# Two recurrent layers with mixtures of experts on one core: output product, linear product, decays and keys in other places of the order

## The reference

```
# layer 1
s  = linear attention of xn: q, k = elu(.)+1, 16 heads of 64; kv = k^T v; (q kv) / (q ksum); @ Wout + bout
x2 = xn + softmax attention of rmsnorm(xn): 16 heads of 8, 4 groups of k and v, rope, causal; @ wo
m  = x2 + sum over the top 2 of 8 experts of w2(silu(w1 h) * (w3 h)) * weight,   h = rmsnorm(x2)
x  = x + s * silu(m)
# layer 2
q, k = l2 normalized; alpha = sigmoid(xn Wg + bg); chunks of 64 tokens:
la = cumsum(log(max(alpha, 1e-6)));  decay = exp(mean la_i - mean la_j) * tril
o  = ((q k^T) * decay) v + (q exp(la)) S;   S = S * exp(la_end) + (k exp(la_end - la))^T v
y  = xn + o Wo;  s = y + gelu(layernorm(y) W1 + b1) W2 + b2
m  = top 1 of 8 experts: relu(xn W1e + b1e) W2e + b2e
x  = x + s * silu(m)
```

## Time and profile before

| | us |
|---|---|
| time, median of 3 runs | 2266.91 (2261.11 to 2269.20) |
| profiled execution | 2266.75 |
| its span in the profile | 2265.0 |
| PE busy | 1846.0 (81%), 23060 matmuls |
| PEld busy | 1306.2 |
| DVE busy | 1238.1 (55%) |
| ACT busy | 1026.2 (45%) |
| POOL busy | 214.9 (9%) |
| mean granted PE clock | 0.919 |

### The profile page before, as it was taken

How to read it: one execution, slowest core, us unless ns; L and a number is a source line. 1 busy time by engine, 2 the same in 40 slices (tenths; PEclk the granted TensorE clock), 3 DMA queues, 4 the chain that set the end, 5 groups by cost and what they waited for, 6 DMA issues and landing times.

```text
span 2265.0 us, 61259 instructions
## 1 busy us (share of the span) xinstructions
PE 1846.0 (81%) x23060; PEld 1306.2 (58%) x23060; DVE 1238.1 (55%) x3454; ACT 1026.2 (45%) x2306; POOL 214.9 (9%) x235
## 2 busy tenths in 40 slices
PE   6999999998989999957788777887888888888652
PEld 4555555556666666635556555655556665655652
DVE  5566666665666656635446544655545655554412
ACT  2444444443555445534554355444554444455332
POOL 0000000000000000020011011100111100110022
PEclk9888889998998989969989999999999999999987
DMA  3222222222122211230221112110111111111374
GB/s 128 78 86 86 86 86 86 90 87 65 60 66 67 67 49 57 75 107 23 64 67 43 55 57 75 44 39 23 56 58 59 59 38 48 48 46 47 103 241 125
DMA packets 97602, 160.99 MB, mean 71 GB/s; under 512 B 14729, under 2 KB 66057, under 8 KB 94090
## 3 DMA queue, kind: packets, MB, share of 16 engines
q1 hardware_dynamic: 88170, 135.05, 18.2%
q0 software_dynamic: 9248, 23.17, 3.3%
HBM read 96.45 MB, written 61.69 MB: 70 GB/s over the span
## 4 chain that ended last, share of the span: by engine, by line
PE 57%; ACT 14%; DVE 12%; issue 11%; SPq 3%; DMA 1%; another core or an unknown queue 1%; POOL 1%; DVEq 0%; ACTq 0%; POOLq 0%
PE psum L907 5%; PE psum L977 4%; PE psum L775 3%; PE psum L897 3%; PE psum L946 3%; PE psum L1218 3%; PE psum L797 3%; PE psum L999 2%; PE psum L1109 2%; PE psum L992 2%; PE psum L1056 2%; PE psum L1080 2%; PE psum L806 2%; PE psum L1147 2%; PE psum L1207 2%
## 5 line engine op out<-in xcount | busy, mean ns | idle before, releaser
L1436 ACT ACTIVATE pts<-psum 128x512 f32<-128x512 f32 x192 | 99.0, 603 | 179.8 <-PE psum L946 179.8
L1901 DVE TENSOR_REDUCE mneg<-psum 128x2 f32<-128x512 f32 (+1 forms) x192 | 119.1, 683 | 57.0 <-PE psum L926 35.2
L682 POOL DMA_INDIRECT rows<-h,recA x64 | 61.8, 965 | 909.6 <-DVE recA L1664 777.5
L797 PE MATMUL psum<-txT,wt 128*128 128x128 f32 x864 | 124.2, 290 | 5.0 <-ACT txT L1319 4.9
L907 PE MATMUL psum<-wa,xT_s 128*128 128x512 f32 x256 | 118.7, 606 | 2.2 <-DVE mneg L1901 2.2
L797 PEld LDWEIGHTS psum<-txT,wt 128*128 128x128 f32 x864 | 113.5, 204 | 10.2 <-ACT txT L1319 6.7
L1066 PE MATMUL psum<-xT_s,wa 128*128 128x256 f32 x512 | 117.5, 383 | 0.0
L706 POOL DMA_INDIRECT rows<-xn,recC x32 | 32.7, 1023 | 884.2 <-DVE recC L2087 762.4
L1066 PEld LDWEIGHTS psum<-xT_s,wa 128*128 128x128 f32 x512 | 94.7, 190 | 25.4 <-issue 13.8
L2015 DVE TENSOR_SCALAR reg<-psum 128x512 f32<-128x512 f32 x16 | 11.1, 692 | 159.2 <-PE psum L1103 159.1
L806 PE MATMUL psum<-wt,tg 128*128 128x128 f32 x528 | 82.3, 288 | 14.4 <-DVE tg L1631 14.4
(11 more groups left out here) (276 smaller groups left out, 4542.8 us busy)
## 6 DMA issues: line engine op xcount, KB each, us to landing
wt<-in_wB SPq DMA_DIRECT2D x84, 384.0 KB, 2.9
outs<-pbd SPq DMA_DIRECT2D x16, 1024.0 KB, 7.0
wt<-in_wD SPq DMA_DIRECT2D x24, 578.0 KB, 3.5
wa<-in_wD SPq DMA_DIRECT2D x15, 578.0 KB, 3.5
tx<-rows SPq DMA_DIRECT2D x132, 64.0 KB, 2.9
outs<-ty SPq DMA_DIRECT2D x132, 64.0 KB, 1.6
rows<-pbd SPq DMA_DIRECT2D x64, 128.0 KB, 1.8
rows<-pbd SPq DMA_DIRECT2D x8, 1024.0 KB, 3.9
```

What stands on the lines that cost most here:

```text
L797: last = mm(bank(f"th{j}")[:, c * P:(c + 1) * P], view[s][:, c * P:(c + 1) * P], txT[:, s, :], start=True, stop=True)
L1436: af(pT[:, n, :], bank(f"e{n}"), ACT.Exp, scale=float(HD) ** -0.5).then_inc(*frees(f"e{n}"))
L1901: ins = v.tensor_reduce(mneg[:, int(n >= 4), col:col + hs], sc, AX.X, ALU.max, negate=True)
```

## The change

Layer 1. The product `wo` with the addition that gives x2 goes from the end of an element to the next one: on PE between `v9` and the k products, on DVE between the copy of v9 and the second pair of queries. A new semaphore `aT_ready` stands for the scaled sums, and x2_ready belongs to stage G. The first scores go ahead of h turned, the v products ahead of the gate. Behind the third scores PE does the linear product first, then the turned maxima, the first numerators, transposed scores 1, tile step 3, transposed scores 2, the second numerators. DVE adds the linear product's bias before the maxima, and divides the second numerators behind the choice and the norm. ACT takes the second set of exponentials ahead of tile step 3.

Layer 2. The logarithms (`decays`) stand right behind z's exponentials, ahead of tile step 4. The key products `lk` of an element are issued in the tail of the element before, behind f0 and f1 and ahead of tile step 5. Their squares are taken by ACT in the new `first_k()`, behind the reload of the table after the gelus, and the copies are now made by DVE, in the new `keys_turned()`, behind the decay means. The sums of squares wait for both.

The list of bank uses follows the new orders. The diff, cut to its core:

```diff
 # PE, layer 1
+            def attention_output():
+                if "G" not in now["stages"]:
+                    return
+                pe.wait_ge(*given("aT_ready", 0))
+                pe.wait_ge(*emptied("wo"))
+                for t in range(NT):
+                    for r in range(GR):
+                        last = mm(bank("wo")[:, t * P:(t + 1) * P], aT[:, r, t * P:(t + 1) * P], woR[:, r, :], start=(r == 0), stop=(r == GR - 1))
+                last.then_inc(*fills("wo"))
...
                 last.then_inc(*fills("v9"))
+                attention_output()
                 tokens("k", INNER)
-                h2_turned()
                 pe.wait_ge(*given("rope_ready"))
                 scores(0)
+                h2_turned()
+                tokens("v", 2 * INNER)
                 gate()
-                tokens("v", 2 * INNER)
...
                 scores(2)
+                linear_output()
+                maxima(1)
                 pe.wait_ge(*given("q0_ready"))
                 numerators(0)
-                linear_output()
-                maxima(1)
+                scores_T(1)
+                tile_step(3)
+                scores_T(2)
                 numerators(1)
-                tile_step(3)
-                scores_T(1)
-                scores_T(2)
...
-                pe.wait_ge(*read_out("pn1"))
...
                 tile_step(7)
 # PE, layer 2
-                products("lk", INNER)
                 tile_step(0)
                 pe.wait_ge(*given("sq_done", 0))
-                pe.wait_ge(*given("sk_done", 4))
-                for j in range(4):
-                    pe.wait_ge(*read_out(f"lk{j}"))
+                pe.wait_ge(*given("sk_done", 0))
+                pe.wait_ge(*given("kT_ready", 0))
...
+                if "P" in now["stages"]:
+                    products("lk", INNER)
                 tile_step(5)
 # ACT, layer 1
                 outputs_turned(1)
+                scores_T(1)
                 tile_step(3)
-                scores_T(1)
                 scores_T(2)
 # ACT, layer 2
+            def first_k():
+                if "P" not in now["stages"]:
+                    return
+                for j in range(4):
+                    act.wait_ge(*filled(f"lk{j}"))
+                    af(sqK[:, 2 * j:2 * j + 2, :], bank(f"lk{j}").rearrange("p (a n) -> p a n", a=2), ACT.Square).then_inc(*signals("sk_done"))
...
-                for j in range(4):
-                    act.wait_ge(*filled(f"lk{j}"))
-                    src = bank(f"lk{j}").rearrange("p (a n) -> p a n", a=2)
-                    af(sqK[:, 2 * j:2 * j + 2, :], src, ACT.Square).then_inc(*signals("sk_done"))
-                    af(kT[:, 2 * j:2 * j + 2, :], src, ACT.Copy).then_inc(*frees(f"lk{j}"))
...
                 z_products(0)
                 z_products(1)
+                decays(0)
+                decays(1)
                 tile_step(4)
                 first_q(0)
                 rstd("ln2", small[:, 1:4:2], small[:, 4:6], 1.0, eps)
                 for j in range(1, 4):
                     first_q(j)
-                decays(0)
-                decays(1)
...
                 act.preload_act_table_set("natural_log_exp_and_others")
+                first_k()
                 tile_step(5)
 # DVE
+            def keys_turned():
+                if "P" not in now["stages"]:
+                    return
+                for j in range(4):
+                    dve.wait_ge(*given("sk_done", j + 1))
+                    v.tensor_copy(kT[:, 2 * j:2 * j + 2, :], bank(f"lk{j}").rearrange("p (a n) -> p a n", a=2)).then_inc(*frees(f"lk{j}"))
+                dve.wait_ge(*read_out("lk3"))
+                dve.sem_inc(*signals("kT_ready"))
...
+            def attention_output():
+                if "G" not in now["stages"]:
+                    return
+                dve.wait_ge(*filled("wo"))
+                dve.wait_ge(*given("recA_stored", 1, 16))
+                v.tensor_tensor(x2[:, :, :], xk[:, :, :], tok(bank("wo")[:, 0:N]), ALU.add).then_inc(*frees("wo"))
+                dve.wait_ge(*read_out("wo"))
+                dve.sem_inc(*signals("x2_ready"))
...
-                v.tensor_copy(xk[:, :, :], xn[:, :, :]).then_inc(*signals("dve_chain"))
...
-                h2_scaled()
+                attention_output()
+                v.tensor_copy(xk[:, :, :], xn[:, :, :]).then_inc(*signals("dve_chain"))
                 queries(1)
                 head_stats()
+                h2_scaled()
                 maxima(0)
-                gate_taken()
...
+                gate_taken()
...
                 maxima(2)
+                linear_output()
                 maxima_added(1)
                 divided(0)
-                linear_output()
-                divided(1)
                 tile_step(3)
                 choose()
                 head_norm()
+                divided(1)
                 rows_given()
...
                 decay_means(0)
                 decay_means(1)
+                keys_turned()
                 tile_step(5)
```

More of the change, by code:

```diff
@@ L118, in uses_in_order @@
         names += [f"te{t}{c}" for t in range(NT) for c in range(2)]
-        names += [f"lk{j}" for j in range(4)]
         tile_step(0)
@@ L1051, in attention0 @@
                 tile_step(6)
-                pe.wait_ge(*read_out("pn1"))
-                pe.wait_ge(*emptied("wo"))
-                for t in range(NT):
-                    for r in range(GR):
-                        last = mm(bank("wo")[:, t * P:(t + 1) * P], aT[:, r, t * P:(t + 1) * P], woR[:, r, :], start=(r == 0), stop=(r == GR - 1))
-                last.then_inc(*fills("wo"))
                 tile_step(7)
```

40 lines of the change are left out of this document (22 added, 18 removed).

## The result

The changed kernel took 2148.06 us (median of 4 runs, 2147.29 to 2151.40), the kernel before beside it 2264.01: 0.950 of it, 95% interval 0.945 to 0.955. The forecast was 2134. The profiled execution took 2147.45 us, its span 2145.7, which is 119.3 less than the span before. PE is busy for 1774.0 us instead of 1846.0 with the same 23060 matmuls, at a mean granted clock of 0.947 instead of 0.919. So 72 of the 119 us are the same work done faster, and 47 are idle time of PE that is gone.

The account below looks back on a forecast made before the run. The prediction took PE (57% of the chain) as the bound, with time to win in its waits and low clock. Its terms, -38 -8 -5 +2 -80 +12 -16 = -133, took 2266.75 to 2134 us; range 2105 to 2175, 8 in 10 2100 to 2200.

Parts of the forecast that it names:

- (b): Layer 1's very first element, without experts or a wo before it: 8.2 us less and nothing that comes back, -8 us.
- (f): Layer 2 tail: earlier logarithms, lk fills PE's wait for gelus; with tiles +1.7 us each (+12), without -2.0 (-16).
- (c): Layer 1, six elements with six tiles: same reordered chain, mostly eaten by waits and wo's return; -0.8 us each, -5.
- (a): Layer 1, eight elements without tiles: second half 8.2 us shorter, less wo's 1.9 and slowed q's 1.6; -4.8 each, -38.
- R1: Rival, layer 1: the new order pays nothing there, only layer 2 gains; 2183 us, chance 0.12.
- R3: Rival, whole kernel: low clock moves onto dense products, making it slower than before; 2345 us, chance 0.03.
- (e): Layer 2 head, 16 elements: the key products and PE's 1.84 us stall leave; -5.0 us each, -80.
- R2: Rival, layer 2's head: the 80 us won turn into longer instruction issue gaps; 2214 us, chance 0.10.

## Why the prediction was nearly right

The forecast of -133 us was measured as -116 to -119, inside the range; the mechanism was right in layer 1 without tiles and in layer 2's heads. The terms (b) and (f) were off in size and (c) in sign. That the sum came within 14 us of the profiled difference is in part luck: by the table the terms missed by +4.4, +10.1 and +10.6 us one way and by -2.3, -1.9 and -7.3 the other.

**(a) Elements without tiles: right.** Forecast 18.6 us from the end of the scores to q, measured 19.6. DVE's chain ran in the order given, but 0.3 to 0.5 late from its first link (s0's bias at 4.4, not 3.8 to 4.2, because PE waited 0.53 for the turned outputs and the product took 3.8), and the weighted sums began at 11.5, not 10.8. The first half was 31.4 by my terms (27.9, 1.9 and 1.6) and is 29.4 or 31.1. R1's account of wo (3.3 less, 1.9 and 1.6 more, nothing) is what the run with wo back showed, and the run with the old order showed that all of the gain is the order's. R3 fell: the low clock on q cost 1.7 us in five elements, near the 1.6 of (a), and none in three.

**(b) The first element: the base was wrong.** I took 8.2 off 26.8 us, but without experts this element's second half was 24.7 long, and it has no linear product to fill the wait for the maxima. It is now 21.4: -3.6 with the first half.

**(c) With six tiles: -5 forecast, +5.1 measured, and -14.3 between the second traces of both kernels (400.0 and 385.7), from two chips, of which the second has no late signals.** The step itself is seen in the timeline: the choice of experts starts 11.9 us behind the end of the scores, since ACT's second exponentials now stand ahead of tile 2's logistic, and 9.6 with tile step 3 first. I had named that logistic, and priced only DVE's 1.8 us of idle time before it. Behind the end of the scores the order on ACT costs 2.3 us (29.4 with the later reciprocal, 27.0 with tile step 3 first as well) and the late signal of the sums 2.1 (31.2 and 29.1). Ahead of it wo costs 2.4 to 2.7 (33.5 and 33.7 us in the changed kernel, 31.0 with wo back), where I had 1.9.

**(e) Layer 2's head: -5.0 forecast, -5.8 measured** (to the f products, which stood 61.7 us behind the element's start with six tiles and stand at 55.8 now, 56.7 and 50.9 with three). The stall and the keys were sized right (the sums of squares 5.6 us earlier with six tiles, on average); what I left out is, with three tiles, the clock at the element's start. Windows of the first 6 us, before and after:

```profile
1811.00:1817.00 6.00, 6.00 (x32) 1.36 (x36) 1.82 (x6) 2.10 (x5) 0.00 (x0) 0.67 0.13 47
```
```profile
1842.30:1848.30 6.00, 5.97 (x54) 1.94 (x58) 1.81 (x6) 3.85 (x8) 0.00 (x0) 1.00 0.14 49
```

Before, the wait of 3.78 us for the gelus left low clock on w2 and on the next decay products; it is filled, and 54 recorded matmuls go where 32 went. With six tiles the clock of the first 6.8 us was 0.66 and is 0.61, so there it gave nothing. R2 fell: the issue share of the chain is 11% in both, and the gap ahead of an element's first product grew from 3.3 to 4.0 us on average with six tiles, not by the 5.8 won.

**(f) The tail with tiles: +1.7 forecast, +1.6 measured. Without tiles: -2.0 forecast, -0.7 measured.** Here the mechanism was wrong. I had the next element's instructions asked for when the gelus are done. The branch of the loop stands behind the key products in PE's queue, and comes when those are issued: in the changed kernel the gelus end at 1895.95, the branch stands at 1897.09, the last key product starts at 1897.18 and w2 at 1897.40. Before, the gelus ended at 1874.19 and the branch stood at 1874.40. So on average of six turns the branch comes 5.0 us behind the first f product, where it came 5.9: 1.0 earlier, not 2.0. From the branch the first product takes 3.6 to 4.0 us before and 3.6 to 4.4 after, whatever w2 takes, which gives 0.2 back. So w2's 1.9 us of gain mostly became idle time. That the early logarithms are worth 24 us all the same comes by another way than mine, the chain of squares and copies that must end inside that delay.

Two elements of layer 2 kept little of their head's 5.7 us, which no step had. In the one between the two loops, which has no tiles at all, PE waits 8.2 us for ACT's norms, 2.6 before, so the whole element is 2.9 shorter, not 7. In the last one the tiles behind it wait for their rows, 31.9 us in sum and 28.6 before, and 1.7 is left of the 5 forecast.

The squares start 1.30 us behind the start of the table load (1895.97 and 1897.27), and the load 0.02 behind the last gelu. By that the drain of 1.38 us that the Trainium skill (ScalarE: Activation LUTs, What ACT_TABLE_LOAD costs) adds to each switch is not seen here, and the sum was right to go without it.

## What to carry to other kernels

A gain in a stretch that is half idle came from ordering PE's work by what the slowest in-order chain beside it (here DVE's) needs next, and was counted twice: the wait went, and with it the half clock that followed it. Moving a product away from a boundary pays only if nothing else needed it there as cover; test the move and the order apart, since here the order gave all, and the move paid nothing without tiles and cost 2 us with them. At a loop's end count from the branch, and ask both what is issued ahead of it and which banks the next round's first product needs.

## What the runs showed of the hardware

- The length of one idle stretch did not decide the clock behind it. In one trace the granted clock was 0.50 on the q products behind 1.95 to 1.97 us of idle time in five of eight elements, and 1.00 behind 1.95 to 2.22 us in the other three. In layer 2 it was 0.50 behind 1.95 to 2.10 us at all seven such boundaries with the copies on ACT, and behind 2.38 us at two of six with the late logarithms. With the later reciprocal, where PE stands for 0.17 to 0.36 us ahead of q, none of the eight elements without tiles had it at q, and three of the six with tiles had.
- A loop's turn on PE cost 3.6 to 4.0 us from the branch to the first product in layer 2's elements with three tiles in the kernel before, and 3.6 to 4.4 in the changed one, 2.6 to 3.1 of them behind the fetch of instructions. With six tiles it was 3.6 to 4.1 before and 3.6 to 5.2 after.
- The same kernel took 2240.6 to 2270.5 us on four chips. The same element of one kernel took 61.9 and 65.1 us in two executions, with the signal of PE's sums 0.04 or 1.5 us behind their end, and so ACT's start.
